# Second attention of a two-layer decoder: the experts' combination moved into its loop, constant score rows made adjacent, projections cut in pieces

## The chip, the cores and the metric

The kernel runs on one core of a Trainium2 chip. The time is device microseconds (us) of one execution. TensorE is called PE below, VectorE DVE, ScalarE ACT, GpSimd POOL, and SyncE, which here only starts DMAs, SP.

## What is computed

Two decoder layers on x of 8 sequences x 512 tokens x 256 values, all in float32. Each layer adds to x an attention, a cross-attention and a mixture of experts. The change touches the seam between layer 0's experts and layer 1's attention. Cut to that:

```python
x = x + _L0_ffn_ref(_layernorm(x), ...)      # 8 experts, top 2 of them per token, weighted sum
# layer 1 attention: 16 heads of 16, causal, ALiBi bias
kqv = _layernorm(x) @ W_kqv + b_kqv;  k, q, v = split(kqv)
attn = q @ k.T / sqrt(16)
bias = where(j > i, -1e30, slopes[h] * (j - i))
y = softmax(attn + bias) @ v
x = x + y @ W_proj + b_proj
```

## The kernel before

Tokens lie 128 to a tile (P), four tiles (TB) to a sequence, 32 tiles in all; x stays in SBUF as g.x. The kernel is a row of stages, each a block in which every engine runs its own program and waits on semaphores. The layer 0 experts leave their outputs in DRAM (slots_y), one row for each token and choice. Then two blocks of l1_attention follow.

The first block is combine (L1048 to L1110). For each sequence, POOL copies the slot numbers (L1070, L1071) and starts 8 indirect gathers of 128 rows (L1075), 4 tiles by 2 choices; DVE adds each gathered tile, times its share, to x (L1108), all 4 first choices before the 4 second ones. It keeps two sets of buffers. Beside this the same block sets up the attention: SP loads the weights (load, L1704), POOL makes masks (set_masks, L1720), DVE rearranges weights (set_weights, L1751), and ACT fills whole tensors (set_rows, L1733): qs and ks with zeros in all 128 partitions, then the constant rows of them, each fill over 16 heads x 512 columns.

The second block is the attention proper. Scores are made by a product whose contraction runs over partitions: 64 rows of high and low parts of q and k, spread there by DMA (spread_half, L1773, 8 DMAs for each half of the heads), and constant rows: slopes and places in rows 64, 65 and 96, 97 (ROW_J, ROW_I), the row maximum in rows 98 and 99 (ROW_M), zeros between and after. Scores are computed twice: by query (score_by_query, L1834, rows 0 to 97) for the row maxima, which DVE takes with the causal mask (maxima, L2013), and by key (score_by_key, L1852, all 128 rows, plus one 128x128 matmul per tile that adds the causal mask, L1861), from which ACT takes exponentials (L1967).

A sequence has G = 4 groups of 4 heads, and a group has 12 units (UNITS), three score banks to a head. There are two PSUM banks for the scores by query and two for those by key, so each unit waits until the one two before it has been read. On PE (body, L1910) a group is: turn_maxima (one transpose, L1850, which waits for all 12 maxima); the first AHEAD = 2 units by query of the following group; then what else is due: outputs of the group before (L1864, prob times v), project_v in group 0, turn_heads, project_out of the sequence before and the normalisation's transposes for the next sequence in group 1, project_qk for the next sequence in group 2; turn_outputs; and then 12 times score_by_key(u) and score_by_query(u + 2). I call the part from turn_maxima to the first score_by_key the gap of a group, and the part from there to the next turn_maxima its unit phase. The first score_by_key waits for the maxima, which go through ACT (high_maxima), DVE (low_maxima) and two small DMAs (L1791) into rows 98 and 99. Since the groups' order on each engine is written out by hand, a step waits for all that stands ahead of it in its engine's list.

SP's list in a sequence: the two maxima DMAs of group 0, spread_half(b, 1), the maxima DMAs of groups 1 and 2, spread_half(nxt, 0), those of group 3.

## Time and profile before

| what | value |
|---|---|
| median of 3 runs | 2802.58 us (2795.83 to 2807.66) |
| profiled execution, its own time | 2782.93 us |
| its span | 2781.2 us |
| busy: PE, PE weight load, DVE, ACT, POOL | 2299.1, 1655.2, 1209.1, 714.0, 440.0 us |
| TensorE clock granted, mean over the span | 0.911 of full |

Times within the span are counted from its start. The page has a picture of the span in 40 slices, a chain of waits, and groups of instructions; the trace behind it answers for single lines, in order of time, and for stretches. A granted clock of 1.00 is 2.4 GHz and 0.50 is 1.2 GHz. The profiled execution is 13 us shorter than the fastest of the three timed runs, so differences are made against it and then put on the median.

### The profile page before, as it was taken

Reading aid. Unit: us, or ns where it says so; the run is one execution under the profiler, and the core shown is the slowest. Engines: PE = TensorE matmul, PEld = TensorE weight load, DVE = VectorE, ACT = ScalarE, POOL = GpSimd, SP = SyncE. Lnnn points to the kernel's source line nnn. Section 1 sums busy time; section 2 is a strip of 40 time slices with the busy share of each in tenths; the row PEclk is TensorE's granted clock in tenths of the full one; section 3 lists DMA queues with packets and bytes.
Section 4 is the critical chain, followed back from the end, with each engine's and each line's share of the span. In section 5 each row is a group of like instructions: output and inputs, shape, how many; then the busy total and the mean of one; then the engine's idle time right before and its main releaser. Section 6 shows DMA issues by size and latency. Waiting matters only on the chain. (4 is left out here: it accounts for less than half of the span.)

```text
span 2781.2 us, 36907 instructions
## 1 busy us (share of the span) xinstructions
PE 2299.1 (83%) x11022; PEld 1655.2 (60%) x11023; DVE 1209.1 (43%) x3400; ACT 714.0 (26%) x1244; POOL 440.0 (16%) x482
## 2 busy tenths in 40 slices
PE   5887677660799950699999996989999999999998
PEld 3554344450477740466666664767777777777776
DVE  3442787661233323566666662545422222222244
ACT  1211233310011143244444442211112212122121
POOL 1110233217000027000000000011530000000043
PEclk9998899855899985799999998996999999999999
DMA  6000000042122223333333320004411110100033
GB/s 213 0 0 19 1 0 0 8 161 104 63 64 64 64 78 94 61 63 62 61 61 63 67 55 18 5 33 150 166 63 33 32 34 30 34 32 32 29 91 95
DMA packets 122240, 160.20 MB, mean 58 GB/s; under 512 B 20850, under 2 KB 90418, under 8 KB 121906
## 3 DMA queue, kind: packets, MB, share of 16 engines
q1 hardware_dynamic: 109874, 125.66, 16.3%
q0 software_dynamic: 12288, 33.57, 3.8%
q8 instruction: 41, 0.67, 0.1%
q14 instruction: 37, 0.30, 0.0%
HBM read 75.81 MB, written 49.28 MB: 45 GB/s over the span
## 5 line engine op out<-in xcount | busy, mean ns | idle before, releaser
L1502 PE MATMUL e_up_ps<-e_wgu,e_xT 128*128 x1152 | 344.9, 452 | 0.0
L1608 DVE TENSOR_TENSOR e_h<-e_act_g,e_up_ps 128x344 f32<-128x344 f32 x208 | 106.6, 512 | 475.8 <-PE e_ht_ps L1509 439.1
L1502 PEld LDWEIGHTS e_up_ps<-e_wgu,e_xT 128*128 128x128 f32 x1152 | 219.1, 190 | 103.5
L1535 ACT ACTIVATE e_act_g<-e_up_ps 128x344 f32<-128x344 f32 x208 | 95.1, 457 | 674.7 <-DVE e_h L1608 445.7
L2021 DVE CUSTOM_DVE_ANT_0 a_s_ps<-a_s_ps,a_causal 128x512 f32<-128x512 f32 (+3 forms) x512 | 238.3, 520 | 43.8 <-PE a_s_ps L1842 42.6
L1967 ACT ACTIVATE a_prob<-a_st_ps 128x512 f32<-128x512 f32 (+1 forms) x384 | 195.4, 526 | 110.9 <-PE a_st_ps L1861 107.3
L1518 PE MATMUL e_y_ps<-e_wd,e_hT 128*128 x864 | 198.4, 379 | 0.0
L1842 PE MATMUL a_s_ps<-a_ks,a_qs 98*128 98x512 f32 (+3 forms) x512 | 164.2, 373 | 36.9 <-DMA a_ks<-a_lo 20.2
L1518 PEld LDWEIGHTS e_y_ps<-e_wd,e_hT 128*128 128x128 f32 x864 | 158.7, 190 | 18.5
L1457 POOL DMA_INDIRECT e_wgu<-slots_y,slot x64 | 60.9, 952 | 657.3 <-DMA slots_y<-e_y 609.7
L1859 PE MATMUL a_st_ps<-a_qs,a_ks 128*128 128x512 f32 (+3 forms) x512 | 163.5, 349 | 1.1 <-ACT a_prob L1967 0.4
L1502 PE MATMUL e_up_ps<-e_own_gu,e_xT 128*128 128x344 f32 x512 | 158.8, 465 | 5.9 <-DVE e_xT L1548 5.7
L1204 PE MATMUL e_h_ps<-e_w,e_xT 128*128 x288 | 137.4, 600 | 2.7 <-DVE e_xT L1238 2.7
L1230 ACT ACTIVATE e_hT<-e_ht_ps 128x512 f32<-128x512 f32 x72 | 43.0, 597 | 366.6 <-PE e_ht_ps L1210 366.6
L1219 PE MATMUL e_y_ps<-e_w,e_hT 128*128 x576 | 136.1, 380 | 0.0
L1502 PEld LDWEIGHTS e_up_ps<-e_own_gu,e_xT 128*128 128x128 f32 x512 | 99.7, 196 | 55.6 <-DVE e_xT L1548 6.5
L1842 PEld LDWEIGHTS a_s_ps<-a_ks,a_qs 98*128 98x128 f32 x512 | 88.4, 193 | 73.8 <-DVE a_most L2021 42.5
L1861 PE MATMUL a_st_ps<-a_causalT,a_ident_r 128*128 128x128 f32 x512 | 113.9, 235 | 0.0
L1187 PE MATMUL e_xt_ps<-ident,e_xin 128*128 128x128 f32 x144 | 28.1, 277 | 102.2 <-DMA e_xin<-slots_x 102.2
L1219 PEld LDWEIGHTS e_y_ps<-e_w,e_hT 128*128 128x128 f32 x576 | 104.0, 190 | 11.1
L137 PE MATMUL a_work<-ident,a_xn 128*128 128x128 f32 x64 | 9.6, 297 | 112.5 <-DVE a_xn L125 106.1
L1859 PEld LDWEIGHTS a_st_ps<-a_qs,a_ks 128*128 128x128 f32 x512 | 96.7, 189 | 7.9 <-ACT a_prob L1967 4.6
(376 smaller groups left out, 3951.6 us busy)
## 6 DMA issues: line engine op xcount, KB each, us to landing
e_xin<-slots_x SPq DMA_DIRECT2D x144, 128.0 KB, 2.0
slots_y<-e_y SPq DMA_DIRECT2D x144, 128.0 KB, 1.7
slots_x<-zero_row SPq DMA_DIRECT2D x1, 9216.0 KB, 27.0
e_w<-in_L_ffn_w SPq DMA_DIRECT2D x16, 512.0 KB, 9.8
a_qs<-a_hi SPq DMA_DIRECT2D x32, 256.0 KB, 4.7
a_ks<-a_hi SPq DMA_DIRECT2D x32, 256.0 KB, 4.7
a_qs<-a_lo SPq DMA_DIRECT2D x32, 256.0 KB, 6.1
a_ks<-a_lo SPq DMA_DIRECT2D x32, 256.0 KB, 7.4
```

What stands on the lines that cost most here:

```text
L1204: last = pe.matmul(h_ps[:, j, :], xT[:, j, k * P:(k + 1) * P], w1[:, e, k, :], start=k == 0, stop=k == KT - 1)
L1219: last = pe.matmul(y_ps[:, j, 0:D], hT[:, j, c * P:(c + 1) * P], w2[:, e, c, :], start=c == 0, stop=c == C - 1)
L1457: pool.indirect_dma_start(fetched_rows[place // 4][:, place % 4, c, :], None, g.slots_y, bass.IndirectOffsetOnAxis(ap=g.slot[:, t, c:c + 1 ...
L1502: last = pe.matmul(up_ps[:, 2 * half_ + u_, 0:H], xT[:, j, k * P:(k + 1) * P], up[:, k, u_, half_ * H:(half_ + 1) * H], start=k == 0, stop ...
L1518: last = pe.matmul(y_ps[:, 0:D], hT[:, j, c * P:(c + 1) * P], down[:, c, :], start=c == 0, stop=c == C - 1)
L1535: act.activation(act_g[:, :], up_ps[:, 2 * half_, 0:H], ACT.Silu).then_inc(gated, 1)
L1608: dve.tensor_tensor(h[:, half_ * H:(half_ + 1) * H], act_g[:, :], up_ps[:, 2 * half_ + 1, 0:H], ALU.mult).then_inc(h_kept, 1)
L1842: last = pe.matmul(s_ps[:, u % 2, off:off + (t + 1) * P], qs[0:ROW_M, head, t * P:(t + 1) * P], ks[0:ROW_M, head, 0:(t + 1) * P], start=Tr ...
L1859: pe.matmul(st_ps[:, u % 2, off:off + S - t * P], ks[:, head, t * P:(t + 1) * P], qs[:, head, t * P:], start=True, stop=False)
L1861: last = pe.matmul(st_ps[:, u % 2, off:off + P], ident_r[:, :], causalT[:, :], start=False, stop=True)
L1967: act.activation(prob[:, u // 3, (u % 3) * BANK:(u % 3) * BANK + cols], st_ps[:, u % 2, 0:cols], ACT.Exp).then_inc(exp_done, 1)
L2021: last = dve.tensor_tensor_reduce(s_ps[:, u % 2, off:off + cols], s_ps[:, u % 2, off:off + cols], causal[:, S - cols:], 1.0, -3.0e38, ALU. ...
```

## The change

- combine as a block of its own goes. In the attention's block POOL gathers sequence 0 and 1 before the loop and sequence b + 2 within body b (stage, gather), into one set of buffers (c_rows); DVE adds sequence b + 2 at the ends of groups 2 and 3 (combine(following, ...)), 4 tile products after each. The loop driver is new (over_sequences_ahead).
- The constant rows become rows 64 to 69, adjacent. So score_by_query contracts over 68 rows and score_by_key over 70. Nothing is zeroed. DVE fills 6 partitions of qs from placed and of_head (4 heads, then 12 heads), ACT 6 partitions of ks, head by head.
- The value bias bv is no longer added to v: PE multiplies it with W_proj once (bv_wide, 4 matmul instructions) and DVE adds the product to b_out. keep_values becomes a copy on ACT.
- AHEAD goes from 2 to 5. project_qk, project_v, project_out and outputs are cut in pieces that alternate with the 5 units by query in each gap. project_qk of the next sequence is split between groups 1 and 2; project_out moves from group 1 to group 3. The first of the 5 units stands ahead of turn_maxima. DVE's and ACT's lists are reordered to match.
- The causal matmuls (L1861) stay.

The core of the diff:

```diff
-    AHEAD = 2
+    AHEAD = 5
-    ROW_J, ROW_I, ROW_M = PARTS, 96, 98
+    ROW_J, ROW_I, ROW_M, ROWS = PARTS, PARTS + 2, PARTS + 4, PARTS + 6
-        combine(nc, g, "m0", beside=dict(sync=load, gpsimd=set_masks, scalar=set_rows, vector=set_weights))
...
         @block.gpsimd
+            stage(0)
+            for t in range(TB):
+                gather(0, t)
+            pool.memset(v[:, :, :, HD:], 0.0).then_inc(ready, 1)
...
             norm.gpsimd(0)
+            stage(1)
+            for t in range(TB):
+                gather(1, t)
+            def body(b, nxt, following):
+                if nxt is not None:
+                    norm.gpsimd(nxt)
+                if following is not None:
+                    stage(following)
+                    gather(following, 0)
...
         @block.tensor
-                    pe.matmul(st_ps[:, u % 2, off:off + S - t * P], ks[:, head, t * P:(t + 1) * P], qs[:, head, t * P:],
+                    pe.matmul(st_ps[:, u % 2, off:off + S - t * P], ks[0:ROWS, head, t * P:(t + 1) * P], qs[0:ROWS, head, t * P:],
...
+            pe.wait_ge(consts, CONSTS)
+            for k in range(KT):
+                last = pe.matmul(m_ps[:, 0:D], bv_wide[:, k, :], w_out[:, k, :], start=k == 0, stop=k == KT - 1)
+                    ahead(0)
                     turn_maxima(b, gr)
                     if gr == 0:
-                        project_v(b)
+                        project_v(b, 0)
+                        ahead(1)
+                        project_v(b, 1)
+                        output(0)
+                        ahead(2)
+                        output(1, 2)
+                        ahead(3)
...
+                    if gr == 3:
+                        if not first:
+                            project_out(b - 1, 0, nxt)
+                        ahead(1)
...
                     for u in range(UNITS):
                         score_by_key(b, gr, u)
-                        if following[0] is not None and u + AHEAD < UNITS:
-                            score_by_query(*following, [u + AHEAD])
+                        if u + AHEAD < UNITS:
+                            ahead(u + AHEAD)
...
         @block.vector
+            combine(0, range(TB))
+            stats(0)
+            dve.tensor_tensor(qs[PARTS:ROWS, GH:, :], placed[PARTS:ROWS, 0, :].unsqueeze(1).broadcast_to([ROWS - PARTS, HEADS - GH, S]),
+                              of_head[PARTS:ROWS, 0, GH:].unsqueeze(2).broadcast_to([ROWS - PARTS, HEADS - GH, S]), ALU.add).then_inc(rows_set, 1)
             norm.vector_rows(0)
+            dve.tensor_copy(causalT[:, :], causalT_f[:, :]).then_inc(consts, 1)
...
+                    maxima_ahead(0)
                     low_maxima(b, gr)
+                    maxima_ahead(1, 2)
+                    if gr == 0 and nxt is not None:
+                        stats(nxt)
...
+                    maxima_ahead(*range(6, UNITS))
+                    if following is not None and gr >= 2:
+                        combine(following, range(2 * (gr - 2), 2 * (gr - 2) + 2))
```

## Rows read from the trace of the kernel before

**Rows 1.** The page's span in 40 slices (PE busy and granted clock, tenths).
```profile
PE   5887677660799950699999996989999999999998
PEclk9998899855899985799999998996999999999999
```

**Rows 2.** Order of time, all engines, from the first gather to the first maxima.
```profile
1022.01 1.01 POOL L1075 DMA_INDIRECT m_rows<-slots_y,m_slot  x1 [0.86 <-POOL m_share L1071]
1034.81 2.07 DVE L1108 SCALAR_TENSOR_TENSOR x_rows<-m_rows,m_share,x_rows 128x256 f32<-128x256 f32 x5 [1.93 <-DMA m_rows<-slots_y,m_slot]
...
1116.29 1.41 DVE L94 BATCH_NORM_STATS2 a_stats<-x_rows 128x6 f32<-128x256 f32 x4 [1.65 <-PEq L1052]
...
1120.44 1.94 PE L137 MATMUL a_work<-ident,a_xn 128*128 128x128 f32 x8 [106.14 <-DVE a_xn L125]
...
1123.58 9.75 PE L1822 MATMUL a_work<-a_xnT,a_w_qk 128*128 128x512 f32 x16 [1.20 <-ACT a_xnT L146]
...
1154.30 0.38 PE L1850 MATMUL a_m_ps<-ident,a_most 128*16 128x128 f32 x1 [0.69 <-DVE a_most L2021]
```

**Rows 3.** Groups by line, shapes apart: xcount | busy us, mean ns | idle.
```profile
L671 DVE SCALAR_TENSOR_TENSOR c_cap<-c_mask,c_cap 128x2048 f32<-128x2048 uint8 x1 | 2.3, 2293 | 0.0
...
L1842 PE MATMUL a_s_ps<-a_ks,a_qs 98*128 98x512 f32 x128 | 63.5, 496 | 21.6 <-DMA a_ks<-a_lo 20.2 <-DVE a_most L2021 0.6
...
L1859 PE MATMUL a_st_ps<-a_qs,a_ks 128*128 128x512 f32 x128 | 59.6, 466 | 0.3
```

**Rows 4.** Stretches: us, busy (x) of PE, PEld, DVE, ACT, POOL; PEclk, DMA, GB/s.
```profile
1315.37:1325.98 10.61, 10.61 (x56) 4.87 (x57) 4.00 (x10) 3.56 (x8) 0.00 (x0) 1.00 0.11 28
1325.98:1334.77 8.79, 7.62 (x48) 6.32 (x46) 7.45 (x29) 6.03 (x12) 0.00 (x0) 1.00 1.07 203
1334.77:1342.13 7.36, 5.33 (x40) 2.22 (x41) 1.80 (x7) 1.34 (x4) 0.00 (x0) 0.77 0.03 6
1342.13:1350.22 8.09, 7.66 (x48) 6.30 (x47) 6.79 (x28) 5.58 (x11) 0.00 (x0) 1.00 0.00 0
1350.22:1357.33 7.11, 7.11 (x56) 4.96 (x57) 4.68 (x20) 1.26 (x4) 1.02 (x1) 1.00 0.54 120
1357.33:1365.35 8.02, 7.66 (x49) 6.34 (x47) 7.26 (x29) 5.50 (x11) 0.00 (x0) 1.00 0.88 157
1365.35:1375.32 9.97, 8.91 (x73) 6.60 (x73) 4.36 (x13) 2.44 (x6) 2.36 (x1) 1.00 0.01 2
1375.32:1383.45 8.13, 7.68 (x49) 6.27 (x47) 6.90 (x28) 6.33 (x12) 0.00 (x0) 1.00 0.00 0
1315.37:1383.45 68.08, 62.58 (x405) 43.88 (x405) 43.24 (x163) 32.03 (x63) 3.37 (x2) 0.97 0.32 63
```

**Rows 5.** Order of time, PE, the gap of group 3 and two reference bursts.
```profile
1336.35 0.80 PE L1842 MATMUL a_s_ps<-a_ks,a_qs 98*128 98x512 f32 x3 [1.30 <-DMA a_ks<-a_lo]
1337.08 3.92 PE L1872 MATMUL a_o_ps<-a_prob,a_v 128*32 128x512 f32 x32
...
1351.13 2.36 PE L1872 MATMUL a_o_ps<-a_prob,a_v 128*32 128x512 f32 x32
1353.42 2.86 PE L1829 MATMUL a_work<-a_w,a_xnT 128*128 128x256 f32 x12
```

**Rows 6.** SP's issues of one spread; stretches (columns of rows 4): spread landing, gathers alone.
```profile
1352.47 0.57 SPq L1782 DMA_DIRECT2D a_qs<-a_hi  x1
...
1357.14 0.67 SPq L1782 DMA_DIRECT2D a_ks<-a_lo  x1
...
1354.00:1363.00 9.00, 8.85 (x51) 7.57 (x50) 6.91 (x29) 4.04 (x9) 1.02 (x1) 1.00 1.07 208
...
1040.00:1100.00 60.00, 0.00 (x0) 0.00 (x0) 18.84 (x42) 26.85 (x4) 44.47 (x56) 0.50 0.33 95
```

**Rows 7.** Last group, by key only: stretch (columns of rows 4), then PE in time order.
```profile
1670.67:1677.70 7.03, 6.15 (x35) 4.70 (x33) 0.68 (x2) 5.55 (x11) 0.00 (x0) 1.00 0.00 0
...
1678.20 4.02 PE L1872 MATMUL a_o_ps<-a_prob,a_v 128*32 128x512 f32 x32 [0.47 <-ACT a_prob L1967]
```

496 lines of the change are left out of this document (261 added, 235 removed).

## The prediction

> **What bounds the kernel now.** I read the page's 40 slices first: PE is busy nearly everywhere but for two holes, the second at slices 15 and 16, where the granted clock falls to 1.2 GHz as well [rows 1]. Then the order of time through that hole. The first gather starts at 1022.0 and the first statistics of the attention at 1116.3; in between, POOL starts 64 gathers, one every 1.27 us (a sequence's 8, its copies and its waits make 11.1 us), and DVE adds behind them. PE has waited 106 us when its first transpose comes at 1120.4; q and k are projected from 1123.6; the first maxima are turned at 1154.3 [rows 2]. So some 100 us of the stage are a serial gather, with the setup hidden beside it, and then 34 us of filling the pipeline.
>
> Third, the stretches of one sequence in the loop, cut at each turn of the maxima and each first score by key [rows 4]. A sequence takes 68.08 us: four gaps of 10.61, 7.36, 7.11 and 9.97 (groups 2, 3, 0, 1; 35.05 together) and four unit phases of 8.79, 8.09, 8.02 and 8.13 (33.03). In the gaps of groups 2 and 0 PE is busy all the time: these are bound by PE's work. In that of group 3 it is busy 5.33 of 7.36 at a mean clock of 0.77: the order of time there shows PE waiting 1.30 us for the spread DMA of the next sequence's q and k, and then 32 output matmuls taking 3.92 us where the same burst takes 2.36 a group later [rows 5]. The clock fell after that idle. The gap of group 1 has 1.06 us of idle. In the unit phases no engine is full: DVE 6.8 to 7.45, ACT 5.5 to 6.3 of 8; PE, DVE and ACT hand two banks back and forth. The last group of the stage, which has no scores by query beside it, shows the price without DVE: 12 units in 7.03 us, 0.59 each [rows 7]. From that the coupled unit is worth (8.05 - 2 x 0.59) / 10 = 0.69 us, since the last two of twelve are uncoupled now.
>
> **The start of the stage.** The combination of six sequences leaves the path, that of sequence 0 stays. In the trace of before its eight products end at 1034.81 + 2.07 = 1036.9 [rows 2]. POOL now has smaller memsets ahead of its first gather and v's, causal's and causalT's after the last; from the 4.1 us that POOL spent from the block's start to the first gather I take 1 us off, so 1035.9. There statistics start, instead of at 1116.3; from statistics to the first projection of q and k passed 7.3 us [rows 2], which would give 1043.2. Four things now stand in between. DVE's fill of 12 heads of qs comes between statistics and rows: 6144 elements in each partition. Six partitions are no cheaper than 128 if the time goes by elements of a partition; the nearest row is a two-input operation of 2048 elements, 2.29 us, so 6.9 us [rows 3]; if the 1.2 us for which DVE waited on POOL's rstd runs under the fill, 5.7. I take 6.9. Second, PE now waits for causalT's cast, which stands behind the rows: 0.2 us. Third, its transposes start when all four row tiles are there and not with the first: 1 us. Fourth, four matmul instructions for the value bias stand ahead of them; 16 of 512 columns took 9.75 us in this cold stretch with their waits [rows 2], so four of half the columns take 1.2 to 1.8 us; 1.7. Sum: 1043.2 + 9.8 = 1053.0 against 1123.6. **-71 us.** Between the ends -67 and -75. The rest of the fill is as before: the spread, its DMAs, and twelve units of maxima at a cold clock. The second gather and combination (8 products, some 4 us of DVE) lie in DVE's wait for that spread. ACT's 16 head fills lie beside the gathers. If POOL's copies and masks had to be paid on the path, it would be their 3 us.
>
> The Trainium skill (SBUF, State Buffer, the section on the shared port) says that a DVE operation with two SBUF inputs and a GpSimd operation that reads SBUF exclude each other for the whole instruction. By that rule rstd comes after the fill and the 6.9 holds; without it 5.7 would. No row here decides.
>
> **The loop, gap by gap.** Three more units by query move into each gap. By columns a head is 1280, and PE takes a bit over 0.5 us for three units when nothing holds it (0.80 us for the first two with their latency [rows 5]; 0.5 to 0.8 are the ends; 0.55 taken). project_v, or project_out, is 16 instructions; 12 take 2.86, so 3.5 for all [rows 5]. project_qk is the rest of group 2's gap, about 6.9 us, and 3.5 of it moves.
> - Group 0: 7.11 + 0.55, less 0.1 of waiting: 7.55.
> - Group 1: 9.97, project_out out, half of project_qk in (about even), + 0.55, and the 1.06 of idle shrinks to half since outputs lie between the transposes and their use: 9.6.
> - Group 2: 10.61 - 3.5 + 0.55 - 0.1: 7.55.
> - Group 3: outputs 2.36, project_out 3.5, units 1.0, transposes 0.6, 0.25 of waiting: 7.7. The 1.30 of DMA wait goes, since the spread of the first half no longer waits for q and k of group 2's gap but for those of group 1's, and with the idle goes the fall of the clock (1.56 us).
>
> Together 32.4, against 35.05: **-2.65.** The way from maxima through ACT, DVE and two DMAs to the first score by key stays hidden: the work in each gap is longer than before in group 3 and not shorter elsewhere.
>
> **The unit phases.** Seven coupled units and five uncoupled: 7 x 0.69 + 5 x 0.59 = 7.8, against 8.05. So three units leave by 0.10 each and cost 0.18 each in a gap: AHEAD = 5 by itself brings nothing, and its gain is cover for DVE. But more of DVE's list stands ahead of its unit 5: group 2's phase is 0.75 longer than the others now because low_qk and normalise come late together [rows 4]. I put 0.4, 0.4, 0.75 and 1.0 (add_to_x) on groups 0 to 3: 33.75 against 33.03, **+0.7.** The ends are 0 (31.2 in all, -1.8) and the double, +3.3. The eight products of the combination (5 took 2.07 [rows 2], so 1.7 for each four) lie in DVE's idle while PE does the five uncoupled units, 3 us.
>
> **The gathers beside the spread.** While a spread lands, the 16 DMA engines are full: 1.07 from 1354 to 1363, 8 issues from 1352.5 to 1357.8; during the gathers alone the share is 0.33, one gather in 1.27 us, so 0.42 us of full engines each [rows 6]. POOL reaches the gathers of b + 2 after rstd, some 8 us into group 0, while spread_half(b, 1) lands until 13.5 us in. Four to five gathers add 1.9 us to it, and group 1's first unit by query needs it 15 us in, 0.3 before the turn of the maxima, which stands behind it in PE's list. So a wait from 0 to 1.4 us; I take **+0.6.** It is the fourth end of a chain that had 1.4 us to spare.
>
> The Trainium skill (DMA: Bandwidth & Descriptors, "Issuing engines are not separate DMA queues") states that DMAs of all engines run on the same 16 and interleave, which speaks against the change here: by it the 1.9 us are paid in full by the spread. Were POOL's queue its own, the term would be 0.
>
> **The sum.** One sequence: -2.65 + 0.7 + 0.6 = -1.35. Six of them: -8. The first, which has no outputs in its first gap and no project_out: -1. The last, whose gaps of groups 0 to 3 lose a project_out from group 1: -3. With the start: -71 - 8 - 1 - 3 = **-83 to -84 us**. The profiled execution had 2782.9, so 2699; the median of the runs shown is 19.7 higher, and I carry the difference onto it: **2719 us**.
>
> **Rivals.**
> 1. *The loop gains in full.* DVE's late steps find room in the uncoupled part and the spread is in time: -1.35 becomes -4.5, and the total is 22 lower: 2697. For it: DVE is busy 43.2 of 68.1 us and gets 4 more for combination less 1.4 for v. Chance 0.17.
> 2. *The late spread lets the clock fall.* If the gathers delay it by 1.5 us or more, PE idles as it does in group 3 now, and the following gap starts at 1.2 GHz: +0.9 and +1.6 a sequence, +18 to 20: 2738. For it: rows 5 and 6. Against: it needs the upper end. Chance 0.13.
> 3. *Narrow matmuls let the clock fall at every group.* The uncoupled tail grows to five units, and after the last group's twelve uncoupled ones the outputs took 4.02 us instead of 2.36, at half the clock [rows 7]. There it took all twelve and 0.47 us of idle. If the 68 and 70 rows in place of 98 and 128 count for the clock too, four falls of 1.65 us in each of 8 sequences cost 53: 2771. Nothing in the trace separates rows: 98 take 496 ns and 128 take 466, with 512 columns [rows 3], which tells of time and not of the clock. Chance 0.08.
> 4. *Slower than before.* The same mechanism without end: the clock stays at 1.2 GHz through the loop. Then the 32 us of gaps double and the unit phases (3072 columns in a head, 2.56 us at 1.2 GHz) reach 41: 105 us for a sequence, +37 x 8 less 71: about 3025. It decides from 77 us a sequence on (68.1 + 71 / 8), that is, when the clock is low for a quarter of the time. Chance 0.03.
> 5. *The start isn't shortened as said,* because a setup step hidden now (weights, constant rows, code) shows: 15 to 60 us lost, 2750. Chance 0.04.
>
> **The numbers.** The forecast has 0.55. Its own range, from the ends above, is 2705 to 2732. The range for 8 in 10 takes in rivals 1 and 2 with the scatter of the runs: 2690 to 2745. Faster by over 0.5% (14 us, about what a measurement of this kernel can tell from no change): all but rival 4 and the tail of 3 and 5, 0.95; within 0.5%: 0.02; slower: 0.03.
>
> **What would show it.** The first projection of q and k some 35 us after the block's start, against 105.7. The fill of 12 heads near 6.9 us between statistics and rows. A sequence of 66 to 67 us, gaps of 7.6, 9.6, 7.6, 7.7 and phases near 8.4. PE's wait for the spread in group 3 gone and a shorter one at group 1. The mean clock in the loop up from 0.97. The prediction is wrong if the loop's sequence is outside 63 to 69 us, or if the start lands outside 1049 to 1057.

## The result

The changed kernel takes **2868.2 us** (median of 4 runs, 2860.2 to 2872.5) against 2805.1 of the kernel before on the same chip (2795.8 to 2811.2): a ratio of 1.0232, 95% interval 1.0214 to 1.0251. The forecast was 2719, range 2690 to 2745. The change makes the kernel slower by 63 us where 86 us of gain were forecast.

In its 40 slices (share of busy PE and mean granted clock, in tenths), the hole of [rows 1] is shorter (TensorE waits 32.8 us in it instead of 106.1), and then the clock stays at 7 tenths for seven slices (17 to 23, counted from 0) where it stood at 9:

```profile
PE   5887677740999939899998997988899999999998
PEclk9998899755999976877777776996999999999999
```

The start of the stage, in order of time, answers to [rows 2]:

```profile
1021.28 1.01 POOL L1703 DMA_INDIRECT a_c_rows<-slots_y,a_c_slot  x1 [0.86 <-POOL a_c_share L1697]
...
1038.98 6.55 DVE L2098 TENSOR_TENSOR a_qs<-a_placed,a_of_head 6x6144 fp32r<-6x6144 f32 x1
1039.04 7.41 POOL L114 TENSOR_TENSOR a_rstd<-a_var_eps,minus_half 128x4 f32<-128x4 f32 x1 [5.12 <-DVE a_var_eps L108]
...
1048.17 2.05 PE L1848 MATMUL a_m_ps<-a_w_out,a_bv_wide 128*128 128x256 f32 x4 [32.82 <-DVE a_causalT L2102]
...
1052.84 7.25 PE L1760 MATMUL a_work<-a_xnT,a_w_qk 128*128 128x512 f32 x16 [1.11 <-ACT a_xnT L146]
...
1080.90 0.41 PE L1788 MATMUL a_m_ps<-ident,a_most 128*16 128x128 f32 x1
```

The first projection of q and k starts at 1052.84 (before: 1123.58), the first maxima are turned at 1080.90 (before: 1154.30). So the start brought 73.4 us (72.7 if each trace is counted from its own first gather, 59.6 against 132.3 us). The rest took it back. One sequence of the loop, cut as in [rows 4] at each turn of the maxima and each first score by key, gap and unit phase of groups 0, 1, 2 and 3 (columns as there):

```profile
1326.36:1336.72 10.36, 10.36 (x61) 6.47 (x59) 5.88 (x27) 1.51 (x4) 1.33 (x3) 0.76 0.66 138
1336.72:1351.30 14.58, 9.63 (x46) 7.75 (x44) 6.26 (x25) 6.29 (x13) 10.11 (x9) 0.66 0.52 120
1351.30:1362.64 11.34, 11.34 (x68) 6.61 (x67) 4.49 (x16) 3.79 (x7) 0.00 (x0) 0.83 0.01 1
1362.64:1371.74 9.10, 8.23 (x45) 6.85 (x44) 5.40 (x21) 6.38 (x13) 0.00 (x0) 0.84 0.00 0
1371.74:1381.32 9.58, 9.58 (x53) 4.57 (x51) 4.54 (x16) 1.86 (x5) 0.00 (x0) 0.80 0.65 138
1381.32:1391.56 10.24, 9.18 (x45) 8.00 (x44) 7.19 (x25) 6.37 (x13) 0.00 (x0) 0.72 0.41 78
1391.56:1401.41 9.85, 9.85 (x60) 6.66 (x59) 3.88 (x15) 1.02 (x3) 0.00 (x0) 0.77 0.01 2
1401.41:1411.78 10.37, 9.28 (x46) 7.72 (x45) 7.57 (x26) 5.99 (x12) 0.00 (x0) 0.74 0.00 2
```

A sequence takes 85.4 us instead of 68.1, and no stretch has the full clock. The fall itself, in finer stretches of group 3's unit phase, the turn, and the next gap:

```profile
1401.41:1403.41 2.00, 2.00 (x16) 1.77 (x15) 1.68 (x6) 1.39 (x3) 0.00 (x0) 1.00 0.00 0
1403.41:1405.41 2.00, 1.17 (x7) 0.87 (x7) 2.00 (x8) 0.69 (x2) 0.00 (x0) 1.00 0.00 0
1405.41:1407.41 2.00, 2.00 (x10) 1.61 (x10) 1.68 (x7) 1.39 (x3) 0.00 (x0) 0.74 0.00 0
1407.41:1409.41 2.00, 1.74 (x8) 1.55 (x7) 1.63 (x7) 1.06 (x3) 0.00 (x0) 0.50 0.01 4
...
1411.78:1416.78 5.00, 5.00 (x17) 3.30 (x18) 1.76 (x7) 0.27 (x2) 0.00 (x0) 0.52 0.14 28
1416.78:1422.10 5.32, 5.32 (x48) 3.16 (x41) 4.12 (x20) 1.24 (x3) 1.33 (x3) 1.00 1.08 226
```

The clock goes from 2.4 to 1.2 GHz (1.00 to 0.50) in the middle of the unit phase, in which TensorE was busy for 6.9 of the first 8 us. It stays there over the turn and the first half of the next gap, and comes back in it. In the sequences of the loop no group is without it: their stretches have mean clocks of 0.66 to 0.89.

The unit phase of group 0 holds a second loss (14.58 us where the others have 9 to 10). TensorE waits twice for nothing that the profile names. The rows of ScalarE beside them say more:

```profile
1341.85 0.31 PE L1799 MATMUL a_st_ps<-a_causalT,a_ident_r 128*128 128x128 f32 x1
...
1344.62 0.60 ACT L1963 ACTIVATE a_prob<-a_st_ps 128x512 f32<-128x512 f32 x1 [2.90 <-PE a_st_ps L1799]
...
1345.27 0.58 PE L1797 MATMUL a_st_ps<-a_qs,a_ks 70*128 70x256 f32 x1 [1.76 <-issue]
...
1347.49 0.60 ACT L1963 ACTIVATE a_prob<-a_st_ps 128x512 f32<-128x512 f32 x1 [2.28 <-remote]
1348.14 0.80 PE L1797 MATMUL a_st_ps<-a_qs,a_ks 70*128 70x512 f32 x1 [2.19 <-issue]
```

The scores that ScalarE exponentiates at 1344.62 were finished by TensorE at 1342.16, 2.5 us before. TensorE, which may be only two units ahead, goes on 0.05 us after that exponential has ended, and again 0.05 us after the next one. So TensorE waits for ScalarE, and what is late is ScalarE, for no reason that the profile names ("remote" is no engine). VectorE is late with it: its maxima of that stretch start at 1344.76 after 1.28 us of the same kind.

**How the traces are compared.** The end of the stage is marked by the first matmul of the cross attention, the next one: 1700.8 before, 1762.8 after, +62.0, the difference of the medians (63.1) within 1 us. Behind that mark no kernel of this study differs in code, yet the rest takes 1080 to 1083 us on some chips and 1099 to 1108 on others (1080.4 in the trace of before, 1103.0 in that of the changed kernel). So whole spans of traces aren't compared below, but the stage's length **L**, from the first turn of the maxima to that mark, and ratios to the kernel before on the same chip. A ratio with an interval comes from repeated runs; "one run" is a single run against the median of before on its chip, and four runs of one kernel differ by up to 17 us (g_late). The 62.0 are made up of: start -73.4; first sequence +16.0 (77.6 against 61.6); the five next +85.5 (424.0 against 338.6); the last with a full body +16.4; the tail +17.5.

| kernel | rows by query / key | units ahead | gathers | L, us | ratio to before |
|---|---|---|---|---|---|
| before | 98 / 128 | 2 | own block | 546.5 | 1 |
| b_key100 | 98 / 100 | 2 | own block | 548.4 | 1.003 (one run) |
| b_dense | 68 / 70 | 2 | own block | 608.9 | 1.0228 (1.0211 to 1.0245) |
| changed kernel | 68 / 70 | 5 | group 0 | 681.9 | 1.0232 (1.0214 to 1.0251) |
| shift64 | 68 / 70 | 5 | group 0 | 655.0 | 1.014 (one run) |
| ahead2 | 68 / 70 | 2 | group 0 | 627.5 | 1.004 (one run) |
| r_key128 | 68 / 128 | 5 | group 0 | 614.4 | 1.021 (one run) |
| r_100 | 98 / 100 | 5 | group 0 | 580.5 | 0.9905 (0.9889 to 0.9920) |
| r_wide | 98 / 128 | 5 | group 0 | 558.3 | 0.9817 (0.9792 to 0.9842) |
| r_wide_ahead2 | 98 / 128 | 2 | group 0 | 557.0 | 0.9810 (0.9782 to 0.9838) |
| r_best | 98 / 128 | 2 | late | 553.4 | 0.9802 (0.9789 to 0.9815) |

### The profile page after: what moved, and what is told of

It reads as the page before. It is cut to its first block and busy times, and to the rows that moved or that the text cites. A ratio compares the mean times of both kernels' runs of the same rounds, so it can differ in the third digit from the quotient of the medians.

```text
span 2865.8 us, 36672 instructions
## 1 busy us (share of the span) xinstructions
PE 2427.4 (85%) x11026; PEld 1745.9 (61%) x11027; DVE 1209.7 (42%) x3391; ACT 685.0 (24%) x1269; POOL 445.4 (16%) x489
## 5 line engine op out<-in xcount | busy, mean ns | idle before, releaser
L1780 PE MATMUL a_s_ps<-a_ks,a_qs 68*128 68x512 f32 (+3 forms) x512 | 209.2, 458 | 35.7 <-DVE a_most L2032 20.6
L1797 PE MATMUL a_st_ps<-a_qs,a_ks 70*128 70x512 f32 (+3 forms) x512 | 213.1, 448 | 30.4 <-issue 17.3
L1780 PEld LDWEIGHTS a_s_ps<-a_ks,a_qs 68*128 68x128 f32 x512 | 111.7, 235 | 101.6 <-issue 52.6
L1797 PEld LDWEIGHTS a_st_ps<-a_qs,a_ks 70*128 70x128 f32 x512 | 125.1, 244 | 46.1 <-ACT a_prob L1963 19.8
L1437 PEld LDWEIGHTS e_up_ps<-e_own_gu,e_xT 128*128 128x128 f32 x512 | 101.0, 199 | 71.0 <-DVE e_xT L1483 15.6
L1799 PE MATMUL a_st_ps<-a_causalT,a_ident_r 128*128 128x128 f32 x512 | 140.4, 281 | 0.0
L1799 PEld LDWEIGHTS a_st_ps<-a_causalT,a_ident_r 128*128 128x128 f32 x512 | 129.6, 253 | 1.8
```

The costliest lines, as they stand in the source:

```text
L1437: last = pe.matmul(up_ps[:, 2 * half_ + u_, 0:H], xT[:, j, k * P:(k + 1) * P], up[:, k, u_, half_ * H:(half_ + 1) * H], start=k == 0, stop ...
L1780: last = pe.matmul(s_ps[:, u % 2, off:off + (t + 1) * P], qs[0:ROW_M, head, t * P:(t + 1) * P], ks[0:ROW_M, head, 0:(t + 1) * P], start=Tr ...
L1797: pe.matmul(st_ps[:, u % 2, off:off + S - t * P], ks[0:ROWS, head, t * P:(t + 1) * P], qs[0:ROWS, head, t * P:], start=True, stop=False)
L1799: last = pe.matmul(st_ps[:, u % 2, off:off + P], ident_r[:, :], causalT[:, :], start=False, stop=True)
```

## The experiments

**The rows.** Theory 1: contracting over 68 and 70 rows instead of 98 and 128 takes TensorE's full clock away. Rival, theory 2: the new order does, above all AHEAD = 5 with its long run of scores by key without others between. The first kernel, r_wide, spreads the rows out again and leaves the order:

```diff
-    ROW_J, ROW_I, ROW_M, ROWS = PARTS, PARTS + 2, PARTS + 4, PARTS + 6
+    ROW_J, ROW_I, ROW_C, ROWS = PARTS, PARTS + 2, PARTS + 4, PARTS + 6
+    ROW_M, S_ROWS, ST_ROWS = 98, 98, 128
...
+            for dst in (qs, ks):
+                sp.dma_start(dst[70:98, :, :]..., g.zero_row[70:98, :]...).then_inc(padded, 16)
+            for dst in (qs, ks):
+                sp.dma_start(dst[100:128, :, :]..., g.zero_row[100:128, :]...).then_inc(padded, 16)
+            sp.dma_start(ks[98:100, :, :]..., g.ones[98:100, :]...).then_inc(padded, 16)
...
-                    last = pe.matmul(s_ps[...], qs[0:ROW_M, ...], ks[0:ROW_M, ...])
+                    last = pe.matmul(s_ps[...], qs[0:S_ROWS, ...], ks[0:S_ROWS, ...])
...
-                    pe.matmul(st_ps[...], ks[0:ROWS, ...], qs[0:ROWS, ...])
+                    pe.matmul(st_ps[...], ks[0:ST_ROWS, ...], qs[0:ST_ROWS, ...])
```

> The changed kernel, but with its constant rows spread out: the two rows of the maxima lie at 98 and 99, the matmuls by query run over 98 rows and those by key over 128 (rows 70 to 97 and 100 to 127 hold zeros), as many rows as in the kernel before. The order of the work and the count of columns stay. If the number of rows decides whether TensorE keeps its full clock (theory 1), the granted clock of the attention stage comes back from some 0.76 to 0.95 to 1.0, a sequence falls from 85 us to 68 to 72, and the total to 2700 to 2740 us. If the order does it, units 0 to 4 without second scores between them and a longer tail of pairs (theory 2), clock and total stay: 2850 to 2880 us. Theory 3 (the gathers stall the units of group 0) speaks only of 4 to 5 us a sequence, which stay in this kernel.

Measured: 0.9817 (0.9792 to 0.9842). The same work in the same order has the full clock in every stretch (groups 0, 1, 2, 3, gap and unit phase):

```profile
1356.78:1364.78 8.00, 8.00 (x61) 5.05 (x59) 5.79 (x27) 1.51 (x4) 1.33 (x3) 1.00 0.37 86
1364.78:1374.26 9.48, 7.38 (x45) 6.01 (x44) 6.04 (x25) 6.46 (x13) 6.83 (x7) 1.00 1.06 233
1374.26:1383.77 9.51, 9.51 (x69) 5.44 (x67) 4.49 (x16) 3.65 (x6) 3.34 (x2) 1.00 0.11 31
1383.77:1392.06 8.29, 7.22 (x45) 5.89 (x44) 5.39 (x21) 6.25 (x13) 0.00 (x0) 1.00 0.00 0
1392.06:1399.72 7.66, 7.66 (x52) 3.65 (x51) 4.54 (x16) 2.00 (x5) 0.00 (x0) 1.00 0.55 122
1399.72:1408.50 8.78, 7.20 (x45) 5.96 (x44) 7.07 (x25) 6.27 (x13) 0.00 (x0) 1.00 0.73 135
1408.50:1416.17 7.67, 7.67 (x60) 5.16 (x59) 3.89 (x15) 1.16 (x3) 0.00 (x0) 1.00 0.01 2
1416.17:1425.36 9.19, 7.45 (x46) 5.98 (x44) 7.57 (x26) 6.02 (x12) 0.00 (x0) 1.00 0.00 2
```

TensorE is busy for 7.2 to 7.5 of 8.3 to 9.5 us in the unit phases, so in groups 1 to 3 it idles more than in the changed kernel, and keeps its clock. What was added is rows of zeros. Theory 1 holds, and a sequence takes 68.6 us against 85.4, or against 81.9 where the stall of group 0 is absent (shift64, below). The zeros aren't free: from the first gather to the first projection r_wide takes 38.8 us and the changed kernel 31.6.

Rows alone, in the old kernel (b_dense copies the four constant rows to 66 to 69 in the setup, puts the maxima at 68 and 69):

```diff
-    ROW_J, ROW_I, ROW_M = PARTS, 96, 98
+    ROW_J, ROW_I, ROW_C = PARTS, 96, 98
+    ROW_M, ROWS = 68, 70
+            for dst in (qs, ks):
+                sp.dma_start(dst[66:70, :, :].bitcast(F32), dst[96:100, :, :].bitcast(F32)).then_inc(dense, 16)
-    pe.matmul(st_ps[...], ks[:, head, ...], qs[:, head, ...]
+    pe.matmul(st_ps[...], ks[0:ROWS, head, ...], qs[0:ROWS, head, ...]
```

> The kernel before with the dense rows alone: its four constant rows are copied to rows 66 to 69 in the setup, the maxima go to rows 68 and 69, and the matmuls run over 68 rows by query and 70 by key. Order, AHEAD = 2 and combination are those of before. Theory 1 (rows decide on the clock, whatever the order): the clock of the attention stage falls from 0.97 to 1.0 to about 0.8, as in the changed kernel with AHEAD = 2, a sequence from 68 to 76 to 79 us, and the total rises by 60 to 90 us. Rival, rows matter only under the new order with its matmuls in pieces: the clock stays over 0.93 and the total within 20 us of before.

Measured: 1.0228 (1.0211 to 1.0245); a sequence takes 75.0 us. This one edit, which saves no instruction and no matmul time, costs as much as the whole change, +64.7 us. Five of its eight stretches (gap and phase of group 2, gap and phase of group 3, gap of group 1), to be read beside [rows 4]:

```profile
1341.26:1351.87 10.61, 10.61 (x56) 4.87 (x57) 4.00 (x10) 3.56 (x8) 0.00 (x0) 1.00 0.11 29
1351.87:1362.16 10.29, 9.38 (x48) 8.37 (x47) 7.78 (x29) 5.97 (x12) 0.00 (x0) 0.75 0.92 176
1362.16:1368.76 6.60, 5.87 (x43) 2.63 (x42) 1.80 (x7) 1.41 (x4) 0.00 (x0) 0.61 0.01 3
1368.76:1377.85 9.09, 8.97 (x49) 7.86 (x47) 7.01 (x28) 5.43 (x11) 0.00 (x0) 0.79 0.00 0
...
1395.41:1408.16 12.75, 11.69 (x75) 7.92 (x74) 4.36 (x13) 2.51 (x6) 2.36 (x1) 0.77 0.01 1
```

In the old order too the clock falls in three of four unit phases (0.75, 0.79 and 0.77; group 1 keeps 1.00). It isn't the run of uncoupled scores that lets it fall.

Two sizes in between: b_key100 is the kernel before with 100 rows by key, r_100 is r_wide with 100 rows by key.

```diff
-                    pe.matmul(st_ps[...], ks[:, head, ...], qs[:, head, ...]
+                    pe.matmul(st_ps[...], ks[0:ROW_M + 2, head, ...], qs[0:ROW_M + 2, head, ...]
```

> The kernel before with one edit: its matmuls by key run over 100 rows instead of 128 (the 28 rows left out hold zeros, the scores are the same). Nothing moves. If the rows that a matmul runs over bear on the granted clock (theory 1), it falls below the 0.97 to 1.00 of the attention stage, in the unit phases first, and the kernel becomes slower, by something between 20 and 150 us. If rows don't matter (theory 2), nothing changes: 2795 to 2812 us, clock 0.91 over the whole.

Measured: one run, 1.003, L 548.4 against 546.5: nothing that one run can tell. The clock fell in one unit phase of the loop (0.69), and otherwise, as in the kernel before, in the gap of group 3 and at the two ends of the stage. The old order bears 100 rows.

```diff
-    ROW_M, S_ROWS, ST_ROWS = 98, 98, 128
+    ROW_M, S_ROWS, ST_ROWS = 98, 98, 100
```

> The changed kernel with rows 98 by query and 100 by key. If only the total of rows counts, the clock in the stage is close to 1.0 as with 98 and 128, the total at 2725 to 2750 us. If each step down costs under this order, where five units by key run without others between them, the clock falls at some groups: 0.85 to 0.95 in the stage, 2760 to 2820 us.

Measured: 0.9905 (0.9889 to 0.9920), L 580.5, between r_wide's 558.3 and the changed kernel's 681.9. Under the new order the clock falls in some groups (mean 0.74 in some stretches of 20 us, 1.00 in most), so 28 rows of zeros, by key alone, are worth 0.9% here. This is where the order comes in: as far as the one run of b_key100 goes, it makes the kernel more sensitive to rows.

r_key128 is r_wide with wide rows by key alone:

```diff
-    ROW_M, S_ROWS, ST_ROWS = 98, 98, 128
+    ROW_M, S_ROWS, ST_ROWS = 68, 68, 128
```

> The changed kernel with only its matmuls by key over 128 rows (zeros in rows 70 to 127), those by query over 68. Both kinds have as many columns. If the clock goes by the rows of all matmuls together, it comes back in part: mean clock of the stage 0.85 to 0.95, total between 2727 and 2850. If the matmuls by key alone count (in the uncoupled tail of each unit phase there are no others), it comes back in full, 1.0, and the total to some 2730. If the matmuls by query decide, it stays at 0.76 and some 2845.

Measured: one run, 1.021. The expectation overlooked the padding itself: 58 rows brought in two transfers delayed the first turn of the maxima to 1139.1, 54 us behind r_wide. From 1075 to 1115 they moved at 53 GB/s with a DMA share of 0.16, where r_wide's four transfers of 28 rows, about as many bytes in all and in the same pieces of 1 KB, moved at 170 GB/s with a share of 0.95 (1022 to 1045). L is 614.4, between 681.9 and 558.3, and the stall of group 0 is in it, longer than before: those unit phases take 14.9 to 15.6 us from the second to the sixth sequence, r_wide's 8.7 to 9.5. That is most of the 56 us over r_wide. Outside it the clock is back for the most part. Of these two stretches, the unit phase of group 3 in the third sequence still has a fall, and the gap of group 2 in the next has none:

```profile
1357.49:1367.86 10.37, 9.27 (x45) 7.84 (x44) 7.57 (x26) 5.99 (x12) 0.00 (x0) 0.73 0.01 2
1412.72:1420.36 7.64, 7.64 (x52) 3.63 (x51) 4.54 (x16) 2.00 (x5) 0.00 (x0) 1.00 0.55 123
```

In the fourth to sixth sequence groups 2 and 3 and the unit phase of group 1 have 1.00 and the lengths of r_wide, with 68 rows by query; only the gap of group 1, behind the stall, has 0.87 to 0.93. So wide rows by key alone bring back most of the clock. What the 68 rows by query still cost can't be parted from the stall here.

**The order.** ahead2 gives AHEAD = 2 back to the changed kernel: three units by query leave each gap, and VectorE's maxima of units 2 to 5 go behind its normalisations.

```diff
-    AHEAD = 5
+    AHEAD = 2
...
-                    maxima_ahead(1, 2)
+                    maxima_ahead(1)
...
-                    maxima_ahead(3, 4)
...
-                    maxima_ahead(5)
+                    maxima_ahead(2, 3, 4, 5)
```

> The changed kernel with 2 instead of 5 units' maxima taken ahead: the gap between two groups scores units 0 and 1 of the next group by key instead of 0 to 4, and the scores by key of the others go between the pairs of the unit phase. Rows stay narrow (68 by query, 70 by key). Theory 2 (the order lets the clock fall, because the unit phase has less matmul work in its second half): the clock in the unit phase stays up, the mean over the stage rises by 0.1 or more and a sequence falls to some 72 to 76 us. Theory 1 (rows): the clock stays near 0.76, and the total within 40 us of 2868, with whatever the order costs by itself.

Measured: one run, 1.004, L 627.5, a sequence of 78.4 us. The clock stayed low (0.71 to 0.85 in the stretches of a sequence, 0.78 over it), as theory 1 says, but the total fell by 2% of the kernel, some 54 us, more than the 40 that theory 1 left to the order. So with narrow rows AHEAD = 5 costs 27 us, by one run each (655.0 without the stall, against 627.5): a sequence has 42.4 us of gaps and 39.5 of unit phases with five units ahead, 36.4 and 42.0 with two. With wide rows (r_wide and this diff together):

> The changed kernel with spread-out rows (98 by query, 128 by key) and AHEAD = 2, the gathers where the change put them. Against the spread-out rows with AHEAD = 5: in the pair with late gathers, AHEAD = 2 shortened the undisturbed gaps by 1.0 (7.64 to 6.67, 7.68 to 6.71) and left the unit phases alone (8.77 to 8.85, 9.18 to 9.09). If that holds here, a sequence falls from 68.6 to about 65 us and the total by 25 to 30 us, to a ratio of 0.970 to 0.975 against before. If AHEAD = 5 is cover for VectorE, as the prediction said, it stays at 0.98 or rises.

Measured: 0.9810 (0.9782 to 0.9838), the same as r_wide. The expectation had the gaps right (6.7 instead of 7.7 in groups 2 and 3) and missed group 0, for which a sequence takes 70.2 to 71.5 us from the third on, not 65: the unit phase there takes 13.95 us at a mean clock of 0.64, as TensorE stood behind VectorE, which stood in its normalisation and waited for rstd:

```profile
1431.30 1.38 DVE L125 TENSOR_SCALAR a_xn<-x_rows,a_mean,a_rstd 128x256 f32 x4 [1.29 <-POOL a_rstd L114]
...
1433.76 0.79 PE L1787 MATMUL a_s_ps<-a_ks,a_qs 98*128 98x384 f32 x2 [2.50 <-DVE a_most L2040]
```

So "its gain is cover for DVE" was right for one group of four.

**The stall without a name.** Theory 3: the gathers beside the spread starve the units of group 0. g_late starts the gathers of b + 2 only after the maxima of group 1, and adds the output bias before them:

```diff
-                    gather(following, 0)
...
-                    gather(following, 3)
                 pool.tensor_tensor(xb, xb, b_out[:, :]..., ALU.add).then_inc(x_biased, 1)
+                if following is not None:
+                    stage(following)
+                    pool.wait_ge(m_low, b * G + 2)
+                    for t in range(TB):
+                        gather(following, t)
```

> The changed kernel, but with the gathers of the sequence after next moved on GpSimd from group 0's phase to after the low parts of the maxima of group 1, so that they do not run beside the spread of the next sequence. Theory 3: the stall of 4 to 5 us in the units of group 0, in which TensorE and ScalarE wait and no engine is named, comes from the gathers beside the spread: it goes, and the total falls by 4 to 5 us for each of 8 sequences, 30 to 40 us, to about 2830; the granted clock does not rise by it (theories 1 and 2 both leave it at 0.76). If the stall has another cause (the low clock itself, the spread alone) the total stays within 10 us of 2868.

Measured: 1.0172 (1.0143 to 1.0201), a gain of 17 us, half of what was expected; the traced run was the slowest of four, and its L of 678.1 is only 4 us shorter. The unnamed wait went, but TensorE now waited 2.5 us for VectorE at the same place. The same edit in r_wide, and in r_wide with AHEAD = 2:

> The spread-out rows (98 by query, 128 by key) and the later gathers together, in the changed kernel. With the spread-out rows alone TensorE waited 0.57 us for the spread's DMA in the units of group 0. If the gathers make the spread late (the prediction's term of +0.6), this wait goes and a sequence falls from 68.6 to 68.0, the total by 3 to 6 us. If that wait would be there without gathers, nothing changes. The gathers end later and the combination waits for them in groups 2 and 3: if they were late for it, the total would rise by some us a sequence.

> The same with AHEAD = 2 again: three units by query go back from each gap into the unit phase. The unit phases of the spread-out kernel take 8.3, 8.8, 9.2 and 9.5 us, 35.8 a sequence against 33.0 before and 33.75 predicted. If AHEAD = 5 is what lengthens them, since DVE's statistics, products and low parts now stand ahead of its maxima, or since five units run uncoupled, they return to 33 and the gaps shrink by 0.5 each: a sequence near 65, total 25 to 30 us below the other. If AHEAD = 5 gives cover to DVE, as the prediction said, they get longer and the total stays or rises.

Measured: 1.0047 (1.0032 to 1.0062) and 0.9996 (0.9982 to 1.0010), 64 and 50 us worse than r_wide where a gain was expected. Both showed a wait for VectorE in group 0 (2.6 and 3.8 to 4.5 us) and, in the gap of group 1, one of 3.2 and 2.8 to 2.9 us without a name (once put down to ScalarE). Two things had been changed at once, which three kernels took apart. r_wide_bias is r_wide with the addition moved alone:

```diff
+                pool.tensor_tensor(xb, xb, b_out[:, :]..., ALU.add).then_inc(x_biased, 1)
                 if following is not None:
                     stage(following)
                     gather(following, 0)
...
                     gather(following, 3)
-                pool.tensor_tensor(xb, xb, b_out[:, :]..., ALU.add).then_inc(x_biased, 1)
```

r_wide_glate is r_wide with the gathers moved alone, glate2 the changed kernel with that:

```diff
                     stage(following)
-                    gather(following, 0)
...
-                    gather(following, 3)
+                    pool.wait_ge(m_low, b * G + 2)
+                    for t in range(TB):
+                        gather(following, t)
                 pool.tensor_tensor(xb, xb, b_out[:, :]..., ALU.add).then_inc(x_biased, 1)
```

> The changed kernel with spread-out rows and one edit in GpSimd's order: the addition of the output bias to the rows (2.4 us) comes ahead of the gathers, right behind rstd, as in the kernel with late gathers, but the gathers start in the same phase. Theory: GpSimd's addition then runs beside VectorE's normalisation, the two exclude each other, VectorE's maxima come late, TensorE waits some 2.5 us in the units of group 0 and its clock falls there: normalisation 3.3 instead of 1.4 us, that unit phase 12 to 14 us instead of 9.5, the gap after it longer too, total 60 to 90 us over the spread-out rows alone. If the later gathers were the cause instead, this kernel stays within 10 us of 2728.

> The changed kernel with spread-out rows and gathers after the maxima of group 1, but the addition of the bias after them, so away from VectorE's normalisation. If the addition alone made the kernel with late gathers slow, this one is at 2720 to 2730 us with a clock of 0.97 to 1.0 in the stage. If late gathers bring a wait of their own (3.2 us without a named cause at the first projection of q and k in group 1's gap stood in that kernel), that wait is here too, the clock falls behind it, and the total is 2760 or more.

> The changed kernel with its narrow rows, gathers after the maxima of group 1, the addition of the bias after them. The changed kernel waits 4 to 5 us in the units of group 0 with no engine named; with late gathers and early addition that turned into 2.5 us of waiting for VectorE. If the gathers beside the spread cause the first and the addition beside normalisation the second, both are gone here: unit phase of group 0 at about 10.5 us, total 25 to 40 us under the changed kernel, clock in the stage still 0.76. If the unnamed wait stays, it isn't the gathers.

r_wide_bias: one run, 0.992, L 583.3 against 558.3. The addition on GpSimd and the normalisation on VectorE start together, and the latter takes 3.29 us instead of the 1.38 of r_wide (it ends 1.1 us after the addition):

```profile
1385.66 2.38 POOL L1748 TENSOR_TENSOR x_rows<-x_rows,a_b_out 128x1024 f32 x1
1385.88 3.29 DVE L125 TENSOR_SCALAR a_xn<-x_rows,a_mean,a_rstd 128x256 f32 x4
...
1390.25 0.50 PE L1787 MATMUL a_s_ps<-a_ks,a_qs 98*128 98x384 f32 x2 [2.56 <-DVE a_most L2040]
```

TensorE waits 2.56 us and its clock falls: that unit phase takes 12.0 to 13.3 us (clock 0.77 in one of 12.0). The theory of this stall holds; its price of 60 to 90 us was too high, 25 by L. The Trainium skill (SBUF — State Buffer, "Who interferes with whom") says that a VectorE instruction in a two-port mode and a GpSimd instruction exclude each other, and counts tensor_scalar among those that can enter one; the trace agrees.

r_wide_glate: one run, 0.986, L 562.3, 4 us over r_wide; clock 1.00 from the second to the fifth sequence, which take 68.0 to 68.1 us. Late gathers with wide rows neither gain nor cost anything that one run can tell. Alone, then, the two edits cost 25 and 4 us of L, and together, in r_wide_late, 68: the rest lies in the gap of group 1, where neither alone has the wait of 3.2 us. What brings it stays open. glate2: one run, 1.016, L 657.0 and no unnamed wait, as expected: 25 us less than the changed kernel. That looked like proof that the gathers beside the spread cause it. But r_wide has the same gathers beside the same spread and no such wait. So TensorE's code was shifted, by 64 waits that are met already, in TensorE's program ahead of the loop, in the changed kernel and in r_wide:

```diff
+            for _ in range(64):
+                pe.wait_ge(rows_set, 2)
```

> The changed kernel with 64 waits that are met already in TensorE's program ahead of the loop, so that the loop's code lies elsewhere. Theory: the unnamed wait of 4 to 5 us in the units of group 0 is TensorE out of instructions, fetched late while the spread and the gathers fill the DMA engines. Then it moves to another place of the sequence, changes its size or goes, with the packets of the instruction queue at other times. Rival: it belongs to the data (gathers, spread); then it stays at 9 to 11 us behind the first score by key of group 0 with the same 4 to 5 us. The total changes by under 40 us either way.

> The same 64 waits ahead of the loop of the kernel with spread-out rows, which has no unnamed wait. If the place of the code decides, one may appear here, in group 0 or where the loop turns over, with a fall of the clock behind it and a total of 2740 to 2800 us. If the narrow rows (or the low clock) bring it, none appears and the total stays at 2720 to 2735 us.

shift64: one run, 1.014, L 655.0: the wait is gone with all work where it was. The unit phase of group 0 takes 10.09 us instead of 14.58 (gap and phase of group 0), and ScalarE starts the exponential that was 2.5 us late 0.04 us after its scores:

```profile
1402.63:1413.08 10.45, 10.45 (x60) 6.47 (x59) 5.88 (x27) 1.51 (x5) 1.33 (x3) 0.76 0.64 134
1413.08:1423.17 10.09, 9.11 (x45) 7.63 (x44) 6.15 (x25) 6.29 (x13) 7.23 (x8) 0.74 0.68 151
...
1418.14 0.31 PE L1799 MATMUL a_st_ps<-a_causalT,a_ident_r 128*128 128x128 f32 x1
1418.49 0.60 ACT L1965 ACTIVATE a_prob<-a_st_ps 128x512 f32<-128x512 f32 x1 [0.41 <-PE a_st_ps L1799]
```

shift_wide: one run, 0.981, nothing appears. So, by one run, 64 instructions ahead of the loop decide whether the wait is there. The theory on record was that TensorE is out of instructions. In the DMA queues of the stretch 1300 to 1500 us (packets, MB, share), the kernel before fetches nothing for its instructions inside the loop:

```profile
q1 hardware_dynamic: 7644, 12.78, 32.4%
```

and the changed kernel does, four 8 KB packets around each turn of the loop's body and one in its middle:

```profile
q1 hardware_dynamic: 5190, 8.54, 21.3%
q0 software_dynamic: 768, 2.10, 3.8%
q14 instruction: 13, 0.11, 0.2%
```

The Trainium skill (Runtime: NRT & Kernel Launch, "Instruction fetch mechanics") tells of a small instruction memory refilled in blocks by the engine's own DMA queue, and of a stall when a branch leaves it. No run here shows that stall. The packets come, but shift64 and r_wide have them too (14 and 12 in the same stretch) and no wait, none comes between 1338 and 1350, where the two waits lie, and TensorE goes on as soon as ScalarE has ended. So TensorE isn't shown to lack instructions; rather what ScalarE and VectorE wait for reaches them late. Why stays open. Gathers are a condition (in glate2 the wait is gone), not enough alone.

**A faster version.** r_best has wide rows, AHEAD = 2, late gathers with the addition behind them, and VectorE's maxima of units 2 and 3 before the normalisation in group 0; r_mix and r_mix_g keep five units ahead in group 0 and two elsewhere, with late and early gathers. r_best against r_wide_ahead2 (with the gathers as in r_wide_glate):

```diff
                         stats(nxt)
+                    if gr == 0:
+                        maxima_ahead(2, 3)
...
-                    maxima_ahead(2, 3, 4, 5)
+                    maxima_ahead(*range(4 if gr == 0 else 2, 6))
```

> Spread-out rows (98 by query, 128 by key), AHEAD = 2, gathers after the maxima of group 1 with the addition of the bias behind them, and in group 0 VectorE takes the maxima of units 2 and 3 between its statistics and its normalisation. With AHEAD = 2 alone TensorE waited 2.5 us in the units of group 0, since VectorE stood in its normalisation and waited for GpSimd's rstd, and its clock fell: unit phase 13.95 us, next gap 10.7. If this cover is what AHEAD = 5 was worth, the phase falls to about 9.5 and the gap after it to 8.6 with the other three gaps at 6.7 to 7.4: a sequence of 65 us against 68.6, a ratio to before of 0.968 to 0.975. If the wait returns elsewhere, it stays at 0.98.

Measured: 0.9802 (0.9789 to 0.9815), the lowest ratio of the study, 2727.5 against 2783.2 us, within the interval of r_wide. TensorE's wait for VectorE fell from 2.5 to 1.8 us only, and the clock fell with it. r_mix_g against r_wide (r_mix has the late gathers too):

```diff
+                    lead = 5 if gr == 0 else 2
...
-                        if u + AHEAD < UNITS:
-                            ahead(u + AHEAD)
+                        if u + lead < UNITS:
+                            ahead(u + lead, True)
...
-                    maxima_ahead(1, 2)
+                    maxima_ahead(*((1, 2) if gr == 0 else (1,)))
```

> Spread-out rows, five units ahead in group 0 and two in groups 1 to 3, gathers after the maxima of group 1 with the addition of the bias behind them. If the stall behind VectorE's normalisation in group 0 ate the gain of AHEAD = 2, it is gone here: clock 1.0 through the loop, gaps of about 8.0 (group 0), 8.5, 6.7 and 6.7 us, unit phases of 8.9, 8.3, 8.8 and 9.1: a sequence of 65 us against 68.0 to 68.6, a ratio to before of 0.970 to 0.975. If the shorter gaps bring waits in other groups, it stays at 0.98.

> The same with the gathers where the change put them, in group 0. With spread-out rows alone the two places of the gathers differed by 0.6 us a sequence (TensorE's wait for the spread in the units of group 0): 3 to 5 us over r_mix, unless that place costs the clock, then 10 us or more.

Measured: 0.9961 (0.9947 to 0.9976) and 0.9909 (0.9888 to 0.9931), both misses. The waits without a name came back (1.2 and 1.6 us in the gap of group 1 beside the late gathers, 1.3 to 2.4 in the units of group 0 beside the early ones), with 1.1 to 3.6 us of waiting for ACT behind them and a fall of the clock. Their order of work was never tried at another place of the code, so whether it is good stays open.

## Why the prediction was wrong

**The start: right.** Term -71 (ends -67 and -75), measured -70.7 at the first projection of q and k (1052.84; forecast 1053.0), -70.0 from each trace's own first gather, and -73.4 at the first turn. The fill took 6.55 us (6.9 forecast), the four bias matmuls 2.05 (1.7). rstd took 7.41 us beside the fill and ended 0.9 us after it, where it takes 1.04 in the loop: of 6.9 and 5.7 the trace takes the first, as the rule of the Trainium skill (SBUF — State Buffer, "Who interferes with whom") would have it.

**The gaps: right at full clock.** Forecast 7.55, 9.6, 7.55 and 7.7; with wide rows 8.00, 9.51, 7.66 and 7.67, together 32.8 against 32.4.

**The unit phases: mis-sized.** Forecast 33.75, with wide rows 35.74 (9.48, 8.29, 8.78, 9.19): +2.7 against [rows 4] instead of +0.7, inside the upper end of +3.3. The late steps of VectorE cost more than was put on them; 0.57 of it is the wait of the next paragraph. So a sequence at full clock takes 68.6 us, 0.5 more than before, where 66.7 was forecast.

**The gathers beside the spread: right.** +0.6 forecast; TensorE waited 0.57 us for the spread in group 0 of r_wide. In the changed kernel itself the wait can't be seen, as everything there is later.

**First and last sequence: wrong sign.** Forecast -1 and -3. In r_wide the first sequence takes 67.1 us against 61.6 (+5.4), its first unit phase 12.8 at a mean clock of 0.68; the last one with a full body takes 72.6 against 66.2 (+6.4), since there are no gathers left ahead of GpSimd's addition, which meets the normalisation; the tail gains 2.3. The sum was 83 to 84. r_wide's is -63.4 (first turn, each trace from its own first gather) + 5.4 + 2.4 + 6.4 - 2.3 = -51.5, and its ratio of 0.9817 says the same: 51 us off the median of 2805.1. Some 7 of the missing 32 us are the padding's own. So without the loss of clock and the stall the forecast would still have been some 25 us too low, most of it in these two sequences and in the unit phases.

**The rows: the step that failed.** It stands in rival 3: "Nothing in the trace separates rows", a chance of 0.08, and four falls of 1.65 us a sequence, 53 us. The two kinds of matmul take about the same time with 98 and 128 rows, 496 and 466 ns [rows 3], and the forecast let that stand for the clock as well: its main sum has no term for the rows. The runs showed a price instead. b_dense, with the rows alone, is 64.7 us slower than before. The mechanism was named at about half its price: groups 1 to 3 take 2.6 to 3.4 us less each with wide rows (group 1: 20.44 against 17.80; group 3: 20.22 against 16.86), not 1.65, because a fall covers half of the unit phase, the turn and half of the next gap, where rival 3 counted the output matmuls of one gap, [rows 7]. From shift64 to r_wide it is 96.7 us of L. Rival 4 set its point at 77 us a sequence, that is, a low clock for a quarter of the time; the sequence has 85.4 and a mean clock of 0.76, low for about half of it. It came true at a chance of 0.03, not in its own form of a clock that stays low, but as rival 3 with another price. What makes the clock follow the rows isn't known; where between 70 and 100 rows it starts to fall in the old order wasn't run.

**The stall: in no step.** 27 us of L (681.9 less 655.0) come from the waits without a name. The text on record had the gathers in the right place with the right partner, the spread, but knew only of a transfer that lands late. The cause stays open.

## What to carry over

Before making matmuls narrower in their contracted rows, treat the clock as part of the price: a version that keeps the order and only adds rows of zeros tells at once what it is, and here zeros were worth 3.3% (shift64 and shift_wide, one run each), and 4% with the stall that went along. Where a trace shows a resource at full value throughout, as the clock in [rows 4], ask what of the work holds it there and whether the change takes that away. And where the profile names no releaser of a wait, look at which other engine's instruction ended just before the engine goes on: here TensorE's waits without a name ended with ScalarE's exponentials. Adding idle instructions ahead of the loop costs one run and tells whether the place of the code matters; it doesn't tell why.

## What the runs showed of the hardware

- The rows over which a matmul contracts bear on the granted clock, not on the matmul's duration. A matmul by key over 512 columns took 0.48 us at full clock with 70 rows and with 128. At 98 and 128 rows (r_wide) the loop had 1.00 from its second to its sixth sequence (0.89 in the first, 0.93 and 0.95 in the last two), at 68 and 70 about 0.76, with the same instructions, columns and order. In between there were partial losses: 98 and 100 rows cost 0.9% under the new order and nothing that one run can tell under the old.
- With 68 rows by query and 128 by key, groups 2 and 3 had 1.00 in three sequences running (r_key128, one run).
- The extra rows held zeros, and these were enough to keep the clock.
- A normalisation, four instructions on 128 x 256 tiles, took 1.38 us alone and 3.29 beside an addition on GpSimd; rstd took 1.04 alone and 7.41 beside a fill with two inputs.
- Zeros moved at 170 GB/s in four transfers of 28 partitions each (r_wide), and about as many at 53 GB/s in two of 58 (r_key128).
- 64 instructions that do nothing, ahead of the loop, made the changed kernel 27 us shorter by L (one run). Its waits of 1.8 and 2.2 us on TensorE had each ended within 0.05 us of an exponential on ScalarE that had started 2.3 to 2.5 us late.
- The same code behind the attention took 1080 to 1083 us on some chips and 1099 to 1108 on others.
